# Splitting the output product of the last routed experts into three products of rounded high and low parts

## The reference, cut to what matters

```python
def _L3_ffn_ref(hidden_states, router_w, router_b, w1, b1, w2, b2):
    probs = softmax(hidden_states @ router_w + router_b)
    topw, topi = top_k(probs, 4)
    topw = topw / sum(topw)
    c = sum(one_hot(topi, 16) * topw[..., None])
    def body(acc, expert):
        w1e, b1e, w2e, b2e, ce = expert
        hmid = gelu(x @ w1e + b1e)
        return (acc + (hmid @ w2e + b2e) * ce[:, None], None)
```

## Time and profile before

| | us |
|---|---|
| runs, median (lowest to highest) | 2634.86 (2633.92 to 2638.57) |
| profiled execution | 2628.6 |
| its span, first to last instruction | 2626.7 |
| TensorE busy in the span | 2309.9 (88%) |
| VectorE, ScalarE, GpSimd busy | 1432.3, 1134.8, 653.6 |
| block loop of the last stage, in the span | about 2274 to 2586 |

### The profile page before, as it was taken

How to read it: one execution, slowest core, us unless ns; L and a number is a source line. 1 busy time by engine, 2 the same in 40 slices (tenths; PEclk the granted TensorE clock), 3 DMA queues, 4 the chain that set the end, 5 groups by cost and what they waited for, 6 DMA issues and landing times. The chain is left out here.

```text
span 2626.7 us, 42342 instructions
## 1 busy us (share of the span) xinstructions
PE 2309.9 (88%) x15416; PEld 1537.3 (59%) x15416; DVE 1432.3 (55%) x3533; ACT 1134.8 (43%) x1948; POOL 653.6 (25%) x852
## 2 busy tenths in 40 slices
PE   1489998998999999869999998889899799599996
PEld 1377754444445799834444434367665445489995
DVE  6825376885464212177887974756577455511114
ACT  6533335666342111136776774332443334134444
POOL 6110132221211033331101001100256410245551
PEclk8689977999998999968999999779999899699998
DMA  5200122330113299741122101021121210589996
GB/s 192 64 4 1 27 52 41 50 50 17 34 30 118 98 333 331 269 107 25 26 37 38 26 2 50 2 81 57 34 33 20 56 18 2 200 291 353 353 345 235
DMA packets 86594, 269.50 MB, mean 103 GB/s; under 512 B 25306, under 2 KB 44242, under 8 KB 70124
## 3 DMA queue, kind: packets, MB, share of 16 engines
q1 hardware_dynamic: 70708, 233.69, 28.9%
q0 software_dynamic: 15680, 33.12, 3.9%
HBM read 207.95 MB, written 23.94 MB: 88 GB/s over the span
## 5 line engine op out<-in xcount | busy, mean ns | idle before, releaser
L1513 ACT ACTIVATE prob<-st_ps 128x1024 f32<-128x1024 f32 x448 | 412.1, 933 | 216.7 <-PE st_ps L1396 214.3
L1533 DVE TENSOR_REDUCE cmax<-ring 128x1 f32<-128x512 f32 x640 | 401.7, 683 | 73.7 <-PE ring L1404 72.0
L2979 PE MATMUL A<-xbT,w 128*128 128x128 f32 x2512 | 301.4, 276 | 0.3 <-issue 0.3
L2979 PEld LDWEIGHTS A<-xbT,w 128*128 128x128 f32 x2512 | 291.4, 193 | 0.7 <-issue 0.5
L1438 PE MATMUL acc<-prob,v 128*32 128x256 f32 (+2 forms) x3200 | 264.0, 404 | 1.2 <-POOL prob L1338 0.7
L3219 DVE COPY yb<-C 128x256 f32<-128x256 f32 x118 | 50.1, 425 | 283.7 <-PE C L2987 283.7
L2896 POOL DMA_INDIRECT y_rows_dram<-yb,dst x118 | 116.3, 986 | 323.7 <-DVE yb L3219 320.6
L2987 PE MATMUL C<-w,hid 128*128 128x256 f32 x632 | 149.5, 380 | 0.0
L1396 PE MATMUL st_ps<-qst,kst 64*128 64x512 f32 (+3 forms) x560 | 135.9, 483 | 9.6 <-DMA qst<-crow 8.0
L1404 PE MATMUL ring<-kst,qst 48*128 48x512 f32 (+3 forms) x560 | 134.4, 409 | 9.2 <-DVE cmax L1533 6.6
L2883 POOL DMA_INDIRECT xb<-x_rows_dram,src x118 | 115.0, 975 | 99.6 <-DVE src L3189 64.3
(11 more groups left out here) (462 smaller groups left out, 4557.5 us busy)
## 6 DMA issues: line engine op xcount, KB each, us to landing
w<-L3f_W_dram SPq DMA_DIRECT2D x79, 1026.0 KB, 8.7
w<-L1f_W_dram SPq DMA_DIRECT2D x39, 1536.0 KB, 9.2
room<-y_rows_dram SPq DMA_DIRECT2D x8, 1024.0 KB, 9.0
kst<-parts SPq DMA_DIRECT2D x120, 64.0 KB, 2.4
qst<-parts SPq DMA_DIRECT2D x120, 64.0 KB, 2.4
gate<-L2f_gates_dram SPq DMA_DIRECT2D x5, 1536.0 KB, 7.6
first<-parts SPq DMA_DIRECT2D x96, 64.0 KB, 2.4
qT<-dense SPq DMA_DIRECT2D x84, 64.0 KB, 2.4
```

Of the source, the lines that this page charges most:

```text
L1513: act.activation(prob[:, step % PROBS, 2 * p:2 * p + 2, 0:n], st_ps[:, p, :, 0:n], ACT.Exp, scale=scale)\
L1533: dve.tensor_reduce(cmax[:, a, t:t + 1, k0 // CH], spot(key)[:, 0:k1 - k0], AX.X, ALU.max)\
L2979: mm = pe.matmul(A[:, j % 2 * 2 + a, f * TB:(f + 1) * TB], up_w(w[:, j % WB], a, k, f), xbT[:, j % 2, k, :], start=(k == 0), stop=(k == KT ...
```

## The change

For `biased` only, the output product of a block is no longer hid times the down weights in fp32. Both are split into a rounded high part and the rest as a low part, all of type float32r, and C becomes the sum of three products: high times high, high times low weights, low times high weights (12 matmuls of 256 columns). The order of engines:

- ScalarE: `raise_down(j + 1)` rounds the 1024 down weights of the next block, right behind the GELUs of block j and ahead of the gT copies and the diagonals. It waits for the weights' load and, as down_hi has two buffers, for the output product of two blocks before. The GELUs themselves now wait for `hid_low` of two blocks before, in place of the output product.
- VectorE: at the start of each loop pass `part_hid(j)` rounds hid and subtracts, then `lower_down(j + 1)` subtracts the rounded down weights; only then come `hold(j - 1)` and `settle(j - 2)`.
- TensorE: `drop_in_parts` waits for `down_low` and `hid_low`.
- To make room, sc and eq move into env.wide, and xb, yb and hid into env.xT, which is free in this stage.

```diff
-        sc = sbuf(nc, st, "sc", [P, NT, E])
+        sc = env.wide[:, 4 * KT * P:4 * KT * P + NT * E].rearrange("p (t e) -> p t e", t=NT) if biased else sbuf(nc, st, "sc", [P, NT, E])
...
-        xb = sbuf(nc, st, "xb", [P, XB, D])
+        flat_xT = env.xT[:, :, :].rearrange("p k t -> p (k t)")
+        xb = flat_xT[:, 0:XB * D].rearrange("p (x d) -> p x d", x=XB) if biased else sbuf(nc, st, "xb", [P, XB, D])
...
-            act, hid = None, sbuf(nc, st, "hid", [P, 2, NF, TB])
+            act, hid = None, flat_xT[:, (XB + 4) * D:(XB + 4) * D + 2 * NF * TB].rearrange("p (x f n) -> p x f n", x=2, f=NF)
+            hid_hi = sbuf(nc, st, "hid_hi", [P, 2, NF, TB], F32R)
+            hid_lo = sbuf(nc, st, "hid_lo", [P, 2, NF, TB], F32R)
+            down_hi = sbuf(nc, st, "down_hi", [P, 2, NF * D], F32R)
+            down_lo = sbuf(nc, st, "down_lo", [P, 2, NF * D], F32R)
...
+        def down_rows(j):
+            return w[:, j % WB, NW * KT * F:NWE]
...
+            def drop_in_parts(j):
+                pe.wait_ge(s.down_low, j + 1)
+                pe.wait_ge(s.hid_low, j + 1)
+                to = room_c(("drop", j))
+                for f in range(NF):
+                    cols = slice(f * D, (f + 1) * D)
+                    pe.matmul(to, hid_hi[:, j % 2, f, :], down_hi[:, j % 2, cols], start=(f == 0), stop=False)
+                    pe.matmul(to, hid_hi[:, j % 2, f, :], down_lo[:, j % 2, cols], start=False, stop=False)
+                    mm = pe.matmul(to, hid_lo[:, j % 2, f, :], down_hi[:, j % 2, cols], start=False, stop=(f == NF - 1))
+                mm.then_inc(s.down_done, 1)
+
             def drop(j):
+                if biased:
+                    drop_in_parts(j)
+                    return
...
+            def raise_down(j):
+                act_e.wait_ge(w_ready[j % WB], 16 * (j // WB + 1))
+                if j >= 2:
+                    act_e.wait_ge(s.down_done, j - 1)
+                act_e.activation(down_hi[:, j % 2, :], down_rows(j), ACT.Copy).then_inc(s.down_high, 1)
+
+            if biased:
+                raise_down(0)
             turn(0)
...
                     if j >= 2:
-                        act_e.wait_ge(s.down_done, j - 1)
+                        act_e.wait_ge(s.hid_low, j - 1)
...
                     a.then_inc(s.hid_ready, 1)
+                    if j + 1 < NBLK:
+                        raise_down(j + 1)
...
+            def lower_down(j):
+                dve.wait_ge(s.down_high, j + 1)
+                dve.tensor_tensor(down_lo[:, j % 2, :], down_rows(j), down_hi[:, j % 2, :].bitcast(F32), ALU.subtract).then_inc(s.down_low, 1)
+
+            def part_hid(j):
+                dve.wait_ge(s.hid_ready, j + 1)
+                if j >= 2:
+                    dve.wait_ge(s.down_done, j - 1)
+                dve.tensor_copy(hid_hi[:, j % 2], hid[:, j % 2]).then_inc(s.hid_high, 1)
+                dve.wait_ge(s.hid_high, j + 1)
+                dve.tensor_tensor(hid_lo[:, j % 2], hid[:, j % 2], hid_hi[:, j % 2].bitcast(F32), ALU.subtract).then_inc(s.hid_low, 1)
+
+            if biased:
+                lower_down(0)
             for j in range(NBLK):
+                if biased:
+                    part_hid(j)
+                    if j + 1 < NBLK:
+                        lower_down(j + 1)
```

More of the change, by code:

```diff
@@ L2737, in routed_moe @@
         idf = sbuf(nc, st, "idf", [P, NT, K])
-        eq = sbuf(nc, st, "eq", [P, NT, K, E])
+        eq = env.wide[:, 0:NT * K * E].rearrange("p (t k e) -> p t k e", t=NT, k=K) if biased else sbuf(nc, st, "eq", [P, NT, K, E])
         prod = sbuf(nc, st, "prod", [P, NT, K, E])
@@ L2774, in routed_moe @@
         else:
-            act, hid = None, sbuf(nc, st, "hid", [P, 2, NF, TB])
-        yb = sbuf(nc, st, "yb", [P, 4, D])
+            act, hid = None, flat_xT[:, (XB + 4) * D:(XB + 4) * D + 2 * NF * TB].rearrange("p (x f n) -> p x f n", x=2, f=NF)
[3 more added lines that the diff above has]
+            down_lo = sbuf(nc, st, "down_lo", [P, 2, NF * D], F32R)
+        yb = flat_xT[:, XB * D:(XB + 4) * D].rearrange("p (x d) -> p x d", x=4) if biased else sbuf(nc, st, "yb", [P, 4, D])
         room = sbuf(nc, st, "room", [P, RU * PAIR * K * D])
@@ L2796, in routed_moe @@
                      "hid_ready down_done y_kept stored0 stored1 stored2 stored3 got0 got1 got2 got3 got4 got5 got6 got7 "
-                     "g_ready scaled blended mixed measured rooted inverted shifted normed spun kept out_stored")
+                     "down_high down_low hid_high hid_low g_ready scaled blended mixed measured rooted inverted shifted normed spun kept out_stored")
         w_ready = (s.w0, s.w1, s.w2, s.w3, s.w4, s.w5)
```

## The result

The changed kernel takes 2626.2 us (median of 6 runs, 2619.26 to 2630.28), the kernel before beside it 2635.55 us (6 runs, 2633.92 to 2641.06): ratio 0.9961, 95% interval [0.9944, 0.9978], about 9 to 10 us faster. The forecast was 2621 in a range of 2610 to 2637. So the direction and the range held, with the time 5 us above the forecast. Whole runs scatter by 10 us and more, the last stage hardly: so I read this stage by itself, from its first row fetch to the end of the span.

The account below looks back on a forecast made before the run. The prediction took TensorE's time to bound the last stage. Its terms, -26.1 + 3.1 + 5.4 + 1.0 + 1.5 + 1.0 = -14.1 us, gave 2621 us against the median 2634.9, range 2610 to 2637.

Parts of the forecast that it names:

- The product: Output product on TensorE: 12 rounded matmuls take 1.40 us, 0.33 less a block; over 79 blocks -26.1 us.
- the bounds 0.110 and 0.127: Time in us of one rounded 256-column matmul: lower bound near 2.4 GHz, upper with a fixed extra of 0.020.
- The settle region: 16 periods where the output product needs the previous yb copy: they fall only to 4.37 us, +3.1 us given back.
- The last four blocks: End of the stage, where ScalarE also makes the diagonals: its queue reaches 5.0 us a block, +5.4 us.
- The start: First blocks: rounding for block 1 stands ahead of the gT and xbT copies on ScalarE, +1.0 us (0 to 2).
- The queues: DMA loads: 1.313 MB a block must move at 386 GB/s against 352; 0.025 a period, +1.5 us (0 to 2.7).
- GpSimd: GpSimd beside VectorE: its two DMA issues may stretch to 3.4 us a block and just fit, +1.0 us (0 to 6).
- DMA's floor of 3.1 to 3.45: Least time in us that DMA needs per block of the last stage, from measured rates and packet times.
- (1): Rival: VectorE and GpSimd block each other both ways, a block needs 4.3 us; about +43 us, 2678; chance 0.08.
- (2): Rival: rounded product dearer, 0.020 fixed per instruction, 12 take 1.52 us; -4.6 us, 2630; chance 0.15.
- (3): Rival: DMA holds the period at 3.6 us or above, 365 GB/s; -4 us, 2631; chance 0.08.
- (4): Rival: weight operations on ScalarE or VectorE take half again as long beside loads; -8 to +5 us, 2627 to 2640; chance 0.10.

Follow-up runs that it names:

- e2: Changed kernel with VectorE's copy out of C and settle addition ahead of the subtraction of the next down weights: ratio 0.9941 to the kernel before, stage 340.2 us.
- e3: Changed kernel with all 32 diagonals made after the last block's GELU, not eight in each of the last four blocks: ratio 0.9943 to the kernel before.
- e9: Kernel before the change with only the diagonals moved behind the last GELU: 2631.02 us in one run, stage 356.3 us against 356.4.
- e11: Changed kernel with VectorE's copy ahead of the subtraction and late diagonals, repeated on another chip: 2619.32 us, ratio 0.9922 to the kernel before.
- e10: Changed kernel with 16 one-column copies on ScalarE ahead of its first rounding of the last stage: one run, stage 347.2 us.
- e8: Changed kernel, three products kept, loading only the second half of an expert's weights from block 6 on: one run, stage 346.7 us.
- e1: Changed kernel again, unedited, in more rounds: median 2633.61 us of 12 runs, ratio 0.9987 to the kernel before.
- e4: Changed kernel with both VectorE's copy ahead of the subtraction and the diagonals after the last GELU: 2621.81 us, ratio 0.9934 to the kernel before.

## Why the prediction was right, and where it was off

The direction and the range held, the time came out 5 us above the forecast, and the account of what bounds the kernel held too: between 2360 and 2557 the chain of the profile after runs through TensorE alone but for 0.8%. By its own terms, measured in the profile after over the 79 blocks:

- **The product**, taken at -26.1: a plain period fell by 0.296 us, 79 times is -23.4. The spacing was taken at 0.1165 and is 0.1195, 12 of them 1.43 us and not 1.40. It lies between the bounds 0.110 and 0.127, nearer to the value that I had chosen than to the upper one: the extra over 2.4 GHz grows with the width, but less than in proportion (0.020 at 512 columns, 0.013 at 256).
- **The settle region**, taken at +3.1: the 15 periods rose by 0.7 instead of falling by 15 x 0.296, so +5.1. This is the step that failed. "ScalarE rounds those of j+1 once the output product of j-1 is done (1.57)" took 1.57 us from the start of the output product to the rounding. The rows show 1.76 (2322.10 to 2323.86): 0.03 of the 0.19 more is the dearer product, the rest lies between the last matmul and what sees it done. What follows was right in sum, 1.10 + 1.14 + 0.56 = 2.80 for 4.37 - 1.57 = 2.80. So the period of 4.37 became 4.56, above the 4.51 of before. e2 shows that it is this loop and no other: with the order of two operations turned it fell to TensorE's 4.19.
- **The last four blocks**, taken at +5.4: the walk gave 19.0 us to the end, the last copy came at 2575.93, 18.8 us after 2557.12. The tail grew by 4.1, and with the five products' 0.296 booked as gained that is +5.5. e3, e9 and e11 show cause and cure.
- **The start**, +1.0: 0.0 and the two products' 0.6, so +0.6.
- **The queues**, +1.5, and **GpSimd**, +1.0: the 57 plain periods have 2.6 us over 57 x 3.438. 1.4 of these are the stop that e10 looks at, 0.6 another period of 4.03. The median period is 3.44 with light loads too (e8), so DMA's floor of 3.1 to 3.45 did not bind, and GpSimd's stretched fetches did not either: e1 had the same 3.44 without them. That the two terms together come out near is luck; what fills them is mostly the stop, which the prediction does not have. DMA is met in one place that I had not named, the late loads of the last blocks (e1, e3).
- After the last store: +0.2.

The sum is -23.4 + 5.1 + 5.5 + 0.6 + 2.6 + 0.2 = -9.4, for a forecast of -14.1. Nearly all of the 4.7 between them is the product's 2.7 and the settle region's 2.0.

**The rivals.** (1), blocking both ways: wrong in its price, since the two engines do not exclude each other, though single blocks do come in the other direction. The groups of the changed kernel by line (ns min/median/max) show it:

```profile
L3255 DVE TENSOR_TENSOR down_lo<-w,down_hi x79: 1208/1225/1227, 2275.5 to 2569.3; 128x1024 fp32r<-128x1024 f32 x79
```

```profile
L2891 POOL DMA_INDIRECT xT<-x_rows_dram,src x79: 947/1473/1974, 2270.5 to 2553.4; - x79
```

79 differences took 1.21 to 1.23 us whatever GpSimd did, and fetches beside them stretched from 0.97 to as much as 1.97; the plain period did not follow. But the rounding of hid on VectorE is held by GpSimd's issues, by line and in the timeline of the changed kernel:

```profile
L3261 DVE CAST hid_hi<-xT x79: 409/427/668, 2279.5 to 2572.5; 128x512 fp32r<-128x512 f32 x79
```

```profile
2510.30 0.99 POOL L2904 DMA_INDIRECT y_rows_dram<-xT,dst  x1 [1.29 <-DVE xT L3251]
...
2510.85 0.67 DVE L3261 CAST hid_hi<-xT 128x512 fp32r<-128x512 f32 x1 [0.82 <-issue]
```

It takes 0.67 us instead of 0.43 and ends 0.23 after the issue. In the eight profiles with three products every such rounding that began with 0.21 to 0.44 us of an issue left ended 0.22 to 0.23 us after it, and none that began with more left was held. That was 2 of 79 here and 26 of 79 in e4, at most 0.24 us each, and the period stayed 3.44. The Trainium skill, SBUF — State Buffer, section "SBUF: two separate sides", has the shared ports locked so that the other engine is blocked in either direction; the trace agrees for GpSimd, and for VectorE in this rounding, while it shows none in the 79 differences, 52 of which began inside an issue. (2), the dearer product: wrong in its 0.127, but the 0.1195 lies under a third of the way to it and cost 2.7 us. (3), DMA holding the period at 3.6: wrong; 383 to 400 GB/s flowed, and e8 left the median period where it was. (4), copies not hidden: the operations kept their prices at the median (1.06, 1.23, 0.43, 0.69), so wrong in its cause, though the settle period came near the 4.6 that it named. It got there through the order of the queue.

## What to carry to other kernels

As long as an engine's sum of work stays below the period, work that is moved to it costs by its place in the queue and not by its length. Wherever TensorE waits for the end of a loop through other engines, walk that loop as a closed one, with the time from the last instruction's start to what sees it done, and put the operation that frees a buffer ahead of the one that prepares the next block. And look for chores that were free as long as the engine had slack, like the diagonals here, with which ScalarE's sum went to 5.0 us a block: they have to be moved with the change that takes the slack. And where the view names a releaser that cannot be, as in e10, look at when the awaited semaphore was raised before you blame the engine that waits.

## What the runs showed of the hardware

- float32r matmuls of 256 columns with 128 rows follow at 0.1195 us, where fp32 ones took 0.216 each; three rounded products cost 0.83 of one fp32 product (1.43 against 1.73).
- GpSimd's DMA issues are stretched by VectorE's operation with two SBUF operands, which itself keeps its length. The other way round, GpSimd's issue holds VectorE's rounding of hid (one SBUF operand, fp32 to fp32r) by up to 0.24 us when that begins with 0.21 to 0.44 us of the issue left. How often they meet differs between executions: the same kernel had a median fetch of 1.47 us in one execution and 0.97 in another (e1), and in e2 it was the store (median 1.72) and not the fetch (1.03) that met it. The median period was the same 3.44 each time.
- A load of 1 MB that lands in 8.8 us at the median took 16.6 once near the end of the stage, beside row fetches and stores.
- In every profile of the changed kernel TensorE's signal of a finished product came up to 3.0 us late in the same block and ScalarE waited for it; in one of the two of the kernel before it was 0.6. Neither ScalarE's instruction count nor the weights' rate moves the place. With two products, which leave less slack, such waits come many times. Their cause stays open.
